# Four output slots in one tensor in place of two, and scatter-adds in groups of four tiles, in an attention and mixture-of-experts kernel

## What is computed

```python
# x: (4096, 512); wg: (32, 512); w1, v1: (32, 512, 192); w2: (32, 192, 512)
scores = softmax(x @ wg.T)
weights, idx = top_k(scores, 8);  weights = weights / sum(weights)
# rows sorted by expert, then for each expert's rows xs:
h = silu(xs @ w1[e]) * (xs @ v1[e])
ys = h @ w2[e]
out = zeros(T, 512).at[t_s].add(ys * w_s)      # every token gets 8 contributions
# around it: x + layernorm(moe(layernorm(x)))
```

## Time and profile before

| | us |
|---|---|
| median of 3 runs | 2547.92 |
| lowest, highest | 2541.41, 2548.30 |
| the profiled execution | 2549.61 |
| its span, first to last instruction | 2547.9 |
| TensorE busy in the span | 2263.1 |
| VectorE, ScalarE, GpSimd busy | 1574.4, 1305.3, 952.4 |

### The profile page before, as it was taken

One profiled execution on the slowest core, in us unless ns is written; L12 is line 12 of the kernel. 1 busy time (PEld: TensorE's weight loads), 2 busy tenths in 40 slices (PEclk: granted clock), 3 DMA queues, 4 the chain that ended last, 5 costly groups with the idle time before them and its releaser, 6 DMA issues.

```text
span 2547.9 us, 69695 instructions
## 1 busy us (share of the span) xinstructions
PE 2263.1 (89%) x11804; PEld 1931.4 (76%) x11805; DVE 1574.4 (62%) x4968; ACT 1305.3 (51%) x2786; POOL 952.4 (37%) x1130
## 2 busy tenths in 40 slices
PE   7999899999989999982898889878999898989990
PEld 5887588888868888871797788767898787977980
DVE  4455567777767777763465656555565555656546
ACT  3343556666656656641455555444555554555443
POOL 1112025555535555555133333323333332333342
PEclk9999999999999999995899999989999998999995
DMA  3334113232333333336688877777786777877778
GB/s 117 94 114 114 58 34 127 106 125 106 129 125 120 120 112 126 108 114 212 158 138 178 173 156 166 166 197 161 149 155 133 179 152 181 140 175 143 135 137 289
DMA packets 164993, 358.13 MB, mean 141 GB/s; under 512 B 21184, under 2 KB 21184, under 8 KB 164800
## 3 DMA queue, kind: packets, MB, share of 16 engines
q0 software_dynamic: 60224, 144.21, 28.5%
q1 hardware_dynamic: 104704, 213.21, 28.1%
HBM read 178.21 MB, written 179.14 MB: 140 GB/s over the span
## 4 chain that ended last, share of the span: by engine, by line
PE 26%; DMA 12%; issue 6%; SPq 5%; DVEq 2%; ACT 1%; DVE 1%; POOL 1%; ACTq 1%; POOLq 0%
DMA BIG<-sorted_rows 9%; PE bank L465 5%; PE bank L466 5%; PE bank L467 5%; PE bank L454 3%; DMA moe_sum<-X,aidx 3%; SPq L329 2%; PE bank L482 1%; PE bank L483 1%; PE bank L484 1%; PE bank L486 1%; PE bank L485 1%; PE bank L475 1%; ACT BIG L598 1%; SPq L348 1%
## 5 line engine op out<-in xcount | busy, mean ns | idle before, releaser
L1479 POOL DMA_INDIRECT moe_sum<-X,aidx x274 | 428.5, 1564 | 868.3 <-issue 504.4
L959 PE MATMUL bank<-WB,XH 128*128 128x512 f32 x1536 | 478.5, 393 | 0.0
L465 PE MATMUL bank<-WB,XL 128*128 x1096 | 405.2, 370 | 8.8 <-issue 2.9
L466 PE MATMUL bank<-WB,XH 128*128 x1096 | 379.0, 346 | 0.0
L467 PE MATMUL bank<-WB,XH 128*128 x1096 | 378.8, 346 | 0.0
L959 PEld LDWEIGHTS bank<-WB,XH 128*128 128x128 f32 x1536 | 290.5, 189 | 60.0 <-issue 0.5
L959 PE MATMUL bank<-WB,XL 128*128 128x512 f32 x768 | 316.2, 412 | 10.7 <-DVE XL L1266 10.7
L959 PE MATMUL bank<-WB,SH 128*128 128x512 f32 x1024 | 319.0, 393 | 0.0
L1545 POOL DMA_INDIRECT sorted_rows<-srow,pos x256 | 266.4, 1041 | 95.4 <-issue 95.4
L736 DVE SCALAR_TENSOR_TENSOR BIG<-BIG,bank x274 | 95.1, 347 | 322.6 <-ACT BIG L535 234.5
L546 ACT ACTIVATE X<-bank (+1 forms) x276 | 165.1, 598 | 240.7 <-POOLq L845 122.4
(11 more groups left out here) (219 smaller groups left out, 4454.9 us busy)
## 6 DMA issues: line engine op xcount, KB each, us to landing
BIG<-sorted_rows SPq DMA_DIRECT2D x278, 274.0 KB
X<-x_in SPq DMA_DIRECT2D x64, 256.0 KB, 2.8
RAW<-w_in SPq DMA_DIRECT2D x16, 768.0 KB
LATE<-w_in SPq DMA_DIRECT2D x16, 768.0 KB
sorted_rows<-BIG SPq DMA_DIRECT2D x33, 274.0 KB, 5.1
moe_sum<-LATE SPq DMA_DIRECT2D x34, 256.0 KB, 3.0
LATE<-x_in SPq DMA_DIRECT2D x32, 256.0 KB, 3.1
RAW<-wo_in SPq DMA_DIRECT2D x16, 512.0 KB, 3.4
```

Of the source, the lines that this page charges most:

```text
L465: nc.tensor.matmul(eu[s][:, 0:UP], XL[:, s, k, :], wh, start=k == 0, stop=False)
L466: nc.tensor.matmul(eu[s][:, 0:UP], XH[:, s, k, :], wh, start=False, stop=False)
L959: last = nc.tensor.matmul(ps, w, m, start=start and i == 0, stop=stop and i == len(terms) - 1)
L1479: nc.gpsimd.indirect_dma_start(acc_dram[:, :], bass.IndirectOffsetOnAxis(aidx[:, s:s + 1], 0), rows, None, compute_op=ALU.add).then_inc(s_ ...
```

## The change

The output slots, `X`, `XN` and `kvs1` become one tensor `Y` of a little over 2048 columns; the four slots are its four blocks of 512. `X` is slots 0 and 1, `XN` slot 2, `kvs1` lies from slot 3 on. Tile g uses slot g mod 4, and `aidx` has four columns. `s_yf` starts at 5, with the same targets. The GpSimd loop body is written four times in place of twice; each copy waits for the same adds as before. The total is rounded up to a multiple of four, and three spare entries in place of one are written into the columns from which the tile table is summed. `sign` and `keep` move to the end of `BIG`, the two marks to `wg`, and with them ScalarE and VectorE wait for the last logits before the first conversion; GpSimd's wait for the last transposes ahead of `sign` is dropped.

```diff
+YSLOTS = 4
...
-        XF = sb("X", [P, 2 * HID])
-        X = XF[:, :].rearrange("p (i n) -> p i n", i=2)
-        XN = sb("XN", [P, HID])
+        YF = sb("Y", [P, 3 * HID + KV_HEADS * (HEAD_DIM + 1)])
+        X = YF[:, 0:2 * HID].rearrange("p (i n) -> p i n", i=2)
+        XN = YF[:, 2 * HID:3 * HID]
...
-        kvs1 = sb("kvs1", [P, KV_HEADS * (HEAD_DIM + 1)])
+        kvs1 = YF[:, 3 * HID:3 * HID + KV_HEADS * (HEAD_DIM + 1)]
...
-        high_mark, low_mark = XN[:, 0:EXPERTS], XN[:, EXPERTS:2 * EXPERTS]
+        high_mark, low_mark = wg[:, 0, :], wg[:, 1, :]
-        sign, keep = XN[:, 2 * EXPERTS:2 * EXPERTS + 2], XN[:, 2 * EXPERTS + 2:2 * EXPERTS + 4]
+        sign, keep = BIG[:, 4104:4106], BIG[:, 4106:4108]
...
-        aidx = sb("aidx", [P, 2], i32)
+        aidx = sb("aidx", [P, YSLOTS], i32)
...
-                nc.scalar.activation(XF[:, at(0, parity, HID, HID)], PS[:, at(ED, parity, HID, HID)], ACT.Copy).then_inc(s_y, 1)
+                nc.scalar.activation(YF[:, bass.ds(((g + YSLOTS) & (YSLOTS - 1)) * HID, HID)], PS[:, at(ED, parity, HID, HID)], ACT.Copy).then_inc(s_y, 1)
...
+            act.wait_ge(s_lgt, TILES)
...
+            dve.wait_ge(s_lgt, TILES)
...
-            done(nc.vector.tensor_copy(ti[:, 0:1], total))
+            done(nc.vector.tensor_scalar(ti[:, 0:1], total, float(YSLOTS - 1), None, ALU.add))
...
-            done(nc.vector.tensor_scalar(ti[:, 1:2], ti[:, 0:1], 1, None, ALU.arith_shift_right))
+            done(nc.vector.tensor_scalar(ti[:, 1:2], ti[:, 0:1], 2, None, ALU.arith_shift_right))
...
-            done(nc.vector.scalar_tensor_tensor(odd[:, 1:2], odd[:, 0:1], -2.0, total, ALU.mult, ALU.add))
+            done(nc.vector.scalar_tensor_tensor(odd[:, 1:2], odd[:, 0:1], float(YSLOTS), total, ALU.mult, ALU.subtract))
...
-            done(nc.vector.tensor_copy(col[EXPERTS:EXPERTS + 1, 2:3], odd[EXPERTS:EXPERTS + 1, 3:4]))
-            done(nc.vector.memset(col[EXPERTS:EXPERTS + 1, 3:4], float(EXTRA)))
+            for i in range(1, YSLOTS):
+                spare = slice(i * EXPERTS, i * EXPERTS + 1)
+                done(nc.vector.tensor_scalar(col[spare, 2:3], odd[spare, 3:4], float(i - 1), None, ALU.add))
+                done(nc.vector.memset(col[spare, 3:4], float(EXTRA)))
+                if i == 1:
+                    done(nc.vector.tensor_tensor(col[spare, 1:2], odd[spare, 3:4], tn[spare, 3, EXPERTS - 1:EXPERTS], ALU.subtract))
+                else:
+                    done(nc.vector.memset(col[spare, 1:2], 1.0))
...
-                nc.vector.tensor_copy(aidx[:, at(0, parity, 1, 1)], BIG[:, bass.ds(tail_at(g) + (WR + ID_COL - W_COL), 1)]).then_inc(s_aid, 1)
+                nc.vector.tensor_copy(aidx[:, bass.ds((g + YSLOTS) & (YSLOTS - 1), 1)], BIG[:, bass.ds(tail_at(g) + (WR + ID_COL - W_COL), 1)]).then_inc(s_aid, 1)
...
-            pool.sem_inc(s_yf, 3)
+            pool.sem_inc(s_yf, 5)
...
-            with pool.Fori(0, pairs) as p:
-                for s in range(2):
-                    g = 2 * p + s
+            with pool.Fori(0, pairs >> 1) as p:
+                for s in range(YSLOTS):
+                    g = YSLOTS * p + s
...
-                    add_rows(s, X[:, s, :])
-                    if s == 0:
-                        pool.wait_ge(s_add[1], 16 * p + 16)
-                    else:
-                        pool.wait_ge(s_add[0], 16 * p + 32)
+                    add_rows(s, YF[:, s * HID:(s + 1) * HID])
+
+                    pool.wait_ge(s_add[1 - s % 2], 32 * p + (16, 32, 32, 48)[s])
                     pool.sem_inc(s_yf, 1)
...
-                                             compute_op=ALU.add).then_inc(s_add[s], 16)
+                                             compute_op=ALU.add).then_inc(s_add[s % 2], 16)
...
-                        pool.wait_ge(s_xt, 2 * TILES)
```

More of the change, by code:

```diff
@@ L174, in layer @@
         at_tile = bq[0:1, 7 * ES:7 * ES + 3 * AT].bitcast(i32).rearrange("p (i n) -> p i n", i=3)
-        ti = sb("ti", [P, 2], i32)
+        ti = ix8[:, 0:2].bitcast(i32)
         page0 = sb("page0", [P, EXPERTS])
@@ L666, in moe_dve @@
             done(nc.vector.tensor_tensor(tn[:, 3, :], tn[:, 3, :], tn[:, 2, :], ALU.subtract))
-            done(nc.vector.tensor_tensor(odd[:, 2:3], odd[:, 0:1], odd[:, 1:2], ALU.add))
+            done(nc.vector.tensor_scalar(odd[:, 2:3], odd[:, 0:1], float(YSLOTS // 2), None, ALU.mult))
             settled()
```

## The result

| | before | after |
|---|---|---|
| median, 20 runs each on one chip, us | 2546.40 | 2553.47 |
| lowest, highest, us | 2539.11, 2549.60 | 2546.99, 2557.29 |
| the profiled execution, us | 2549.61 | 2553.31 |
| its span, us | 2547.9 | 2551.6 |

The ratio of after to before is 1.0028, with a 95% interval of 1.0021 to 1.0036: the changed kernel is slower by some 7 us. The prediction said 3.5 us faster. Its range holds the time, its direction is wrong.

A forecast was written before the change was run, and what follows sets the result against it. The expert loop, 1253 us, was taken as close to TensorE's own 1137.68 us busy time. -12.9 + 7.8 + 0.6 + 1.0 = -3.5 us took the median from 2547.92 to 2544.4 us; range 2529 to 2560 us.

The forecast's parts named there:

- Part 2: Tile count rounded to a multiple of four: two padding tiles at the expert loop's end, +7.8 us, called certain.
- no gain lies there: At the very end ScalarE waits once more for the slot, but GpSimd issues the last adds as close as possible: 0.
- Part 1: Two more output slots remove slot waits in the expert loop, saving 12.9 us, or 6 if row loads take half.
- four stretches: From 1717.30, 2032.03, 2291.51 and 2339.79 us, short experts' serial adds slow TensorE's tiles; savings 3.4, 2.1, 3.1, 3.2 us.
- no adds on the chain in the four stretches: Sign expected in the profile after: adds no longer stand on the chain that ended last in those places.
- The 1.1 us for single tiles: Estimated saving on single slow tiles elsewhere in the loop, from two tiles lengthened by 0.53 us.
- The upper end of 21 us: Largest slot saving: 12.9 us plus a share of half-clock time after stops, some eight stops shortened by 1 us.
- Part 3: VectorE's six more table operations cost 0.6 us; ScalarE's two more register instructions per copy cost 1 us.
- The stops at changes of expert: Rival, chance 0.18: 22 TensorE stops where experts change lose 0.5 us each and a slow stretch vanishes; 2530 us.
- the slow rhythm: Rival, chance 0.14: row loads 4.13 us apart cost TensorE 0.23 us a tile; 2568 us at 120 tiles locked.
- It does not do what it says: Rival, chance 0.08: GpSimd's serial adds fill four slots too, the wait only moves by two tiles; 2556 us.
- The points that were said to show the forecast right: Profile signs: 276 adds, 3.9 us tiles, slot wait under 15 us, load waits 65 to 85, some 20 slow loads.

## Why the prediction was wrong, point by point

**Part 2 and "no gain lies there": the step that failed.** The two tiles were put at 7.8 us, "certain", and of the end it was said that GpSimd issues the last adds as close as it can. That had been read from the kernel before. The added column of the spare entries was in the diff, it feeds `first`, and `first` is what makes adds serial; the prediction priced the lines that write it (0.6 us for the table) and didn't ask who reads it. From the add of tile 273 to the last pass the change adds 11.7 us: 7.8 and 3.9 more. The padding alone adds 11.3 us at the same place, and 10 us to the time by its ratio. The end was part of this term and was put at nothing beyond the two tiles.

**Part 1: right mechanism, a little too large.** The four stretches were put at 11.8 us; they gave 9.5 in the pair (11.9 to 2.4) and 8.3 on the average over six kernels. What is left are single adds that are late even for four slots: in the fourth stretch the chain of the kernel after still has

```profile
2337.56 4.73 DMA moe_sum<-Y,aidx
2342.29 5.67 DMA moe_sum<-Y,aidx
```

and in the second stretch it has

```profile
2036.57 5.57 DMA moe_sum<-Y,aidx
```

so "no adds on the chain in the four stretches" was wrong for these two. The 1.1 us for single tiles can't be seen. The upper end of 21 us, with its shortened half-clock time, found no support.

**Part 3** is within what can be measured: 1.0011, with an interval that includes 1. From the first comparison of pages to the first load of rows it is 11.7 us after and 11.0 before, 0.7 for the forecast 0.6 (the new table has seven small operations more, not six, by the prediction's own prices 0.67 us); the other 1.5 us by which the loop starts later lie ahead of the table, where the diff changes no work but the place of tensors. Over all ten kernels the first add starts at 1233.1 to 1236.3 us where the tensor `Y` is used and at 1231.0 to 1233.4 where it isn't. That hints at some 2 us for the layout, which the times, with 1.0011, can neither show nor exclude.

**The sum, corrected.** Against the pair's spans: -10.0 in place of -11.9 (parts 1 and the register work), +11.7 in place of +7.8, +2.2 in place of +0.6, and -0.2 in the last pass: +3.7 in place of -3.5. From there to the medians' +7.1 it is the 3.2 us by which the execution that was read lay above its own kernel's median. The prediction allowed 1.7 us for this, from three runs; the 20 runs say 3.2.

**The rivals.** The stops at changes of expert didn't shrink (73.1 us of waits for 75.9). The loads didn't lock into the slow rhythm over more tiles; the stretch that was locked before is locked after, at about the same tiles, and among the experiments it comes and goes with two slots and with four. "It does not do what it says" is out: the slot wait went. All of the mechanisms that were weighed lay in the loop, and the one that decided lay behind it. The points that were said to show the forecast right (276 adds, 3.9 us a tile, a slot wait under 15 us, waits for loads of 65 to 85 us) all came true, and so did the one on loads in the slow rhythm (18); only that on adds on the chain didn't. The sign was wrong none the less, since no point was set for the end of the loop. That the time lies within the range says little for the mechanism: the range reached to 2560 us for the sake of loads in the slow rhythm, which was the same before and after. That is luck.

## What to carry to other kernels

When padding is added, follow each value that it writes to its reader, waits included: work that has nothing behind it costs its latency, not only its throughput (here 3.9 us from tile to tile in the loop, 5.5 to 6.1 us from add to add at the end). Write down the span as a few cuts at common events (first add, last add, next pass) and forecast each cut; a sum over one loop misses what stands after it. And a wait of an engine that isn't the bound tells little: 107 us of it went here and some 5 to 10 us of time with them.

## What the runs showed that had not been expected

- Leaving out the weight loads of 29 experts, 116 DMAs, takes 75 us off with two slots (2548.41 to 2473.08) and 87 us with four (2541.32 to 2453.84; 85 us by the ratios 0.9968 and 0.9634). TensorE's waits for rows fall from 75.9 to 1.0 us, about as much as the time, but the wait alone doesn't price the loads. The loop without the loads (PE, PEld, DVE, ACT, POOL, clock, DMA share):

```profile
1228.00:2406.00 1178.00, 1115.89 (x6258) 988.85 (x6255) 727.61 (x1965) 636.83 (x1419) 424.74 (x272) 0.99 0.74 137
```

  It is 75 us shorter than the 1253 us of the earlier trace rows. For the same matmuls (6253 and 6258 in the records) TensorE is busy 22 us less (1137.68 to 1115.89), at a mean granted clock of 0.99 in place of 0.96, and idle 53 us less (115.3 to 62.1). So the price of these loads is the load of rows that comes late with them and, behind it, matmuls at the lower clock (as the 1.11 us transposes of the earlier trace rows). Whether the load is late through the queue or through the bytes wasn't tried.
- A serial add costs more than its transfer: the adds of the padding tiles start 6.12 and 5.82 us apart, where the landing of the one before takes 5.34 and 4.91 us on the chain; GpSimd needs the rest, 0.8 and 0.9 us, to go from the landing to the next issue.
- Single executions can differ in the loop by as much as this change: first add to the add of tile 273 took 1253.89 us in the kernel before and 1247.91 us in its twin with the layout alone, whose median is 0.11% higher, not lower. 3.6 us of these 6.0 are the slow rhythm of the loads, which the one execution has and the other hasn't.
